# Two chunks of the output product in three rounded passes, with the parts of G made on the way

## The reference, cut to what matters

```python
queries = (query @ Wq + bq).reshape(B, L, H, E)        # H = 16 heads, E = 32
scores = jnp.einsum('blhe,bshe->bhls', queries, keys)  # 32 keys, the same for every b
A = sparsemax(scale * scores)
out = jnp.einsum('bhls,bshd->blhd', A, values)
out = jnp.transpose(out, (0, 2, 1, 3)).reshape(B, L, H * D)
x = layernorm(query + out @ Wo + bo)
# feed-forward: s = x @ Win + bin_; h = relu(s[..., None] * W1 + b1)
# g = einsum('btmh,mh->btm', h, W2) + b2
x = layernorm(x + g @ Wout + bout)
```

## Time and profile before

| What | Value |
|---|---|
| Median of 3 runs (lowest, highest) | 1313.4 us (1311.59, 1316.35) |
| Profiled execution: its own time | 1313.41 us |
| Its span, first to last instruction | 1311.6 us |
| Mean granted TensorE clock | 0.983 of full |
| Busy: TensorE, VectorE, ScalarE, GpSimd | 1248.0, 1133.2, 1068.2, 676.5 us |
| DMA: bytes moved, mean rate | 258 MB, 197 GB/s |

### The profile page before, as it was taken

How to read it: one execution, slowest core, us unless ns; L and a number is a source line. 1 busy time by engine, 2 the same in 40 slices (tenths; PEclk the granted TensorE clock), 3 DMA queues, 4 the chain that set the end, 5 groups by cost and what they waited for, 6 DMA issues and landing times. The chain is left out here.

```text
span 1311.6 us, 25223 instructions
## 1 busy us (share of the span) xinstructions
PE 1248.0 (95%) x5848; PEld 853.4 (65%) x5848; DVE 1133.2 (86%) x4538; ACT 1068.2 (81%) x2285; POOL 676.5 (52%) x1634
## 2 busy tenths in 40 slices
PE   8973899999999999999999999999999999989995
PEld 5642566676766767676776767677676767655552
DVE  3986899899999999999999999999999999966776
ACT  3661865779898888989898888989898888987776
POOL 1431333346555555655565555656555555665654
PEclk9995999999999999999999999999999999999998
DMA  6480785655656556565656656565655656468874
GB/s 203 131 215 17 199 246 192 191 185 171 218 184 216 198 197 206 190 217 182 220 188 208 203 191 214 185 220 183 213 196 199 211 186 216 162 227 281 280 233 104
DMA packets 92181, 258.35 MB, mean 197 GB/s; under 512 B 16067, under 2 KB 16067, under 8 KB 75622
## 3 DMA queue, kind: packets, MB, share of 16 engines
q1 hardware_dynamic: 91862, 256.26, 60.0%
q10 hardware_dynamic: 144, 0.26, 0.1%
HBM read 206.13 MB, written 50.33 MB: 196 GB/s over the span
## 5 line engine op out<-in xcount | busy, mean ns | idle before, releaser
L856 PE MATMUL bank<-G_sb,pT 128*128 128x512 f32 x1024 | 462.5, 594 | 2.8 <-DMA G_sb<-G_of_heads 2.1
L856 PEld LDWEIGHTS bank<-G_sb,pT 128*128 128x128 f32 x1024 | 185.2, 191 | 188.6 <-issue 184.3
L1426 DVE SCALAR_TENSOR_TENSOR acc<-hinge,w2c,acc 128x512 f32<-128x512 f32 x210 | 157.1, 748 | 81.7 <-ACT hinge L1019 80.2
L541 POOL TENSOR_TENSOR shift_sq<-sum,per_row_sq 128x1 f32<-128x1 f32 x244 | 95.2, 390 | 252.4 <-DVE y_sb L1269 250.5
L1376 DVE MAX8 top<-bank 128x8 f32<-128x32 f32 x2048 | 211.8, 178 | 0.0
L749 PE MATMUL bank<-A_hi,xT_hi 128*128 128x512 f32 x512 | 203.3, 397 | 0.0
L751 PE MATMUL bank<-A_hi,xT_lo 128*128 128x512 f32 x512 | 202.7, 396 | 0.0
L750 PE MATMUL bank<-A_lo,xT_hi 128*128 128x512 f32 x512 | 202.6, 396 | 0.0
L1019 ACT ACTIVATE hinge<-s_sb,b1c,w1c 128x512 f32<-128x512 f32 x240 | 192.8, 806 | 0.0
L1075 ACT CAST xT_hi<-bank 128x512 fp32r<-128x512 f32 x127 | 74.1, 584 | 134.8 <-PE bank L751 134.8
L989 ACT ACTIVATE unread<-y_sb,shift_sq 128x512 bf16<-128x512 f32 x244 | 174.5, 715 | 7.7 <-POOL minus_mean L543 7.5
(11 more groups left out here) (164 smaller groups left out, 2461.7 us busy)
## 6 DMA issues: line engine op xcount, KB each, us to landing
G_sb<-G_of_heads SPq DMA_DIRECT2D x128, 1024.0 KB, 5.5
x_sb<-in_L_attn_query_dram SPq DMA_DIRECT2D x128, 256.0 KB, 4.7
y_sb<-in_L_attn_query_dram SPq DMA_DIRECT2D x256, 128.0 KB, 5.4
out_dram<-o_sb SPq DMA_DIRECT2D x230, 128.0 KB, 4.7
G_of_heads<-y_sb SPq DMA_DIRECT2D x64, 256.0 KB, 4.0
out_dram<-y_sb SPq DMA_DIRECT2D x11, 256.0 KB, 3.3
y_sb<-in_L_attn_Wk_dram SPq DMA_DIRECT2D x1, 1024.0 KB, 5.9
y_sb<-in_L_attn_Wq_dram SPq DMA_DIRECT2D x1, 1024.0 KB, 8.1
```

The source lines that it names most:

```text
L541: nc.gpsimd.tensor_tensor(shift_sq[:, par:par + 1], total[:, par:par + 1], per_row_sq[:], ALU.mult).then_inc(s_mean, 1)
L856: mm = nc.tensor.matmul(o_ps[i % 2][:], pT[:, bass.ds(pair_place(turn, i) + (i % H * C + c) * P, P)], G_sb[:, i % GR, c, :], start=(c == 0 ...
L1426: nc.vector.scalar_tensor_tensor(acc[:], hinge[:, k % HR, :], w2c[:, k:k + 1], acc[:], ALU.mult, ALU.add).then_inc(s_acc, 1)
```

## The change

The output product treats some of its four chunks like the score: high and low parts of float32r, in three passes. In tiles 0 to 15 no chunk, in tiles 16 to 31 chunk 1, in tiles 32 to 105 chunks 1 and 3, in tiles 106 to 127 none. For this

- GpSimd makes the parts of the probabilities, `part_hi` and `part_lo`, one slot ahead of the product (`LAG_PART` 22): a copy that rounds and a subtraction, of 128 columns per converted chunk. They stand behind the split and ahead of the means.
- G's parts are made once. While tiles 0 to 15 pass, GpSimd makes the high and the low part of chunk 1 of each head's G (`made_hi` ahead of the means, `made_lo` behind the folds, 512 columns each); with tiles 16 to 31 those of chunk 3. SP stores them to `G_of_heads` (512 KB a tile) one slot later, ahead of its load of G.
- A buffer of the ring has six columns of 512 and the ring three buffers. A load brings 1.0 MB (tiles 0 to 15 and 106 to 127), 1.25 MB (16 to 31) or 1.5 MB (32 to 105). Loads from tile 35 on are issued one slot earlier (`LAG_G` 21); earlier ones keep slot i + 22.
- To have the room, `pT` becomes a ring of 20 blocks (it was 32 blocks' worth), reused block by block (`blocks`), and several small tensors go or move into others; four of the memsets at the start go.
- `shift_sq` goes from the means: ScalarE's square takes minus_mean as bias at scale 1, and ve is var / D + eps in one tensor_scalar.

The diff, cut to its core:

```diff
 LAG_PROB = 9
-LAG_G = 22
+LAG_G = 21
+LAG_PART = 22
 LAG_XB = 22
...
-        GR, STAGES = 2, 2
+        GR, STAGES, SETS = 3, 2, 5
         x_sb = sb("x_sb", [P, XR, D])
         xT_hi = sb("xT_hi", [P, C, P], F32R)
...
+        pT = sb("pT", [P, SETS * C * HPC * P])
+        part_hi = sb("part_hi", [P, 2, 2 * P], F32R)
+        part_lo = sb("part_lo", [P, 2, 2 * P], F32R)
         sum1 = sb("sum1", [P, 2])
...
-        G_sb = sb("G_sb", [P, GR, C, D])
-        V_rep, VT_rep = G_sb[:, 0].rearrange("p c n -> p (c n)"), G_sb[:, 1, 0, :]
-        G_dram = nc.dram_tensor("G_of_heads", [H, P, C * D], F32, kind="Internal").ap()
+        G_sb = sb("G_sb", [P, GR, 6, D], F32R)
+        G_hi = sb("G_hi", [P, 2, D], F32R)
+        V_rep, VT_rep = pT[:, 0:H * P], pT[:, C * C * HPC * P:C * C * HPC * P + D]
+        G_COLS = ((1, "raw"), (3, "raw"), (0, "raw"), (2, "raw"), (1, "hi"), (1, "lo"), (3, "hi"), (3, "lo"))
+        G_dram = nc.dram_tensor("G_of_heads", [H, P, len(G_COLS) * D], F32, kind="Internal").ap()
...
-        def pair_place(turn, i):
-            return (turn + i // UNROLL) % 2 * (H * C * P)
+        blocks, spare = [{(n, c): n * C + c for n in range(C) for c in range(C)}], list(range(C * C, C * C + C))
+        for _ in range(1, TILES // UNROLL):
+            old = blocks[-1]
+            blocks.append({(n, c): old[c - 1, n] if c else spare[n] for n in range(C) for c in range(C)})
+            spare = [old[C - 1, c] for c in range(C)]
+        p_blocks = pT[:].rearrange("p (b a n) -> p b a n", a=HPC, n=P)
+        def block_of(i, c):
+            return blocks[i // UNROLL][i % H // HPC, c]
+        PARTS_MADE = (1, 3)
+        PLAIN_FROM = TILES - 22
+        def parts_of(i):
+            chunks = PARTS_MADE[:i // UNROLL] if i < PLAIN_FROM else ()
+            return sorted(chunks, key=lambda c: block_of(i, c))
+        def plain_of(i):
+            return [c for c in range(C) if c not in parts_of(i)]
+        def parts_before(i):
+            return sum(bool(parts_of(n)) for n in range(i))
+        def made_of(i):
+            return PARTS_MADE[i // UNROLL] if i // UNROLL < len(PARTS_MADE) else None
+        MADE_HI, MADE_LO = 4, 5
+        def made_hi(i):
+            return G_sb[:, i % GR, MADE_HI, :] if i < H else G_hi[:, i % 2, :]
+        def made_lo(i):
+            return G_sb[:, i % GR, MADE_LO, :]
+        def made_stores(i):
+            return sum(16 if n < H else 32 for n in range(i % GR, i + 1, GR))
+        def G_cols(i):
+            wanted = [G_COLS.index((c, "raw")) for c in plain_of(i)]
+            wanted += [G_COLS.index((c, part)) for c in parts_of(i) for part in ("hi", "lo")]
+            assert max(wanted) - min(wanted) + 1 == len(wanted)
+            return min(wanted), max(wanted) + 1
+        def G_of(i, c, kind):
+            return G_sb[:, i % GR, G_COLS.index((c, kind)) - G_cols(i)[0], :]
+        def parts_rows(i):
+            places = [block_of(i, c) for c in parts_of(i)]
+            if len(places) == 1:
+                return slice(places[0], places[0] + 1)
+            return slice(places[0], places[1] + 1, places[1] - places[0])
...
             AHEAD = 2
+            LAG_MADE = LAG_WO + 1
+            def G_loads(n):
+                return [i for i, early in ((n - LAG_G - 1, False), (n - LAG_G, True))
+                        if 0 <= i < TILES and early == (i >= len(PARTS_MADE) * H + GR)]
+            def store_made(i):
+                col = G_COLS.index((made_of(i), "hi"))
+                if i < H:
+                    sp.dma_start(G_dram[i % H, :, col * D:(col + 2) * D],
+                                 G_sb[:, i % GR, MADE_HI:MADE_LO + 1].bitcast(F32).rearrange("p c n -> p (c n)")
+                                 ).then_inc(s_made_st[i % GR], 16)
+                else:
+                    for n, part in enumerate((made_hi(i), made_lo(i))):
+                        sp.dma_start(G_dram[i % H, :, (col + n) * D:(col + n + 1) * D],
+                                     part.bitcast(F32)).then_inc(s_made_st[i % GR], 16)
             def slot(turn, j):
...
+                    i = base + j - LAG_MADE
+                    sp.wait_ge(s_made, i + 1)
+                    store_made(i)
+                for i in G_loads(base + j):
                     h = i % H
-                    if isinstance(turn, int) and base + i < H:
-                        if h == 0:
-                            sp.wait_ge(s_Gmm, PIECES)
-                        if h % HPC == 0:
-                            for r in range(STAGES):
-                                sp.wait_ge(s_Gst[r], 16 * HPC * (h // HPC + 1) * (C // STAGES))
-                    if not isinstance(turn, int) or base + i >= GR:
-                        sp.wait_ge(s_o, base + i - GR + 1)
-                    sp.dma_start(G_sb[:, i % GR].rearrange("p c n -> p (c n)"), G_dram[h]).then_inc(
-                        s_G[i % GR], 16)
+                    if i < H and h % HPC == 0:
+                        for r in range(STAGES):
+                            sp.wait_ge(s_Gst[r], 16 * HPC * (h // HPC + 1) * (C // STAGES))
+                    if i >= GR:
+                        sp.wait_ge(s_o, i - GR + 1)
+                        if made_of(i - GR) is not None:
+                            sp.wait_ge(s_made_st[i % GR], made_stores(i - GR))
+                    first, last = G_cols(i)
+                    sp.dma_start(G_sb[:, i % GR, 0:last - first].bitcast(F32).rearrange("p c n -> p (c n)"),
+                                 G_dram[h, :, first * D:last * D]).then_inc(s_G[i % GR], 16)
                 if in_range(turn, j, LAG_XB):
                     i = j - LAG_XB
...
-            def mean(t0, par, s_rows, total, s_mean, minus_mean, shift_sq, s_shift):
+            def mean(t0, par, s_rows, total, s_mean, minus_mean, s_shift):
                 if not isinstance(t0, int) or t0 >= 3:
                     pool.wait_ge(s_shift, t0 - 2)
                 pool.wait_ge(s_rows, t0)
-                nc.gpsimd.tensor_tensor(shift_sq[:, par:par + 1], total[:, par:par + 1], per_row_sq[:],
-                                        ALU.mult).then_inc(s_mean, 1)
                 nc.gpsimd.tensor_tensor(minus_mean[:, par:par + 1], total[:, par:par + 1], per_row[:],
                                         ALU.mult).then_inc(s_mean, 1)
...
                 pool.wait_ge(s_ve, t0)
                 nc.gpsimd.tensor_tensor(rstd[:, par:par + 1], ve[:], minus_half[:], ALU.pow).then_inc(s_rstd, 1)
-                pool.wait_ge(s_mean, 2 * t0)
+                pool.wait_ge(s_mean, t0)
                 pool.wait_ge(s_rstd, t0)
...
                     pool.wait_ge(s_lo, lead // GROUP + 1)
+                if in_range(turn, j, LAG_PART) and parts_of(base + j - LAG_PART):
+                    i = base + j - LAG_PART
+                    rows = p_blocks[:, parts_rows(i), i % HPC, :]
+                    hi, lo = (part[:, i % 2, 0:len(parts_of(i)) * P].rearrange("p (c n) -> p c n", n=P)
+                              for part in (part_hi, part_lo))
+                    pool.wait_ge(s_p, i // UNROLL * UNROLL + 3 * GROUP + i % H // HPC + 1)
+                    pool.wait_ge(s_o, i - 1)
+                    nc.gpsimd.tensor_copy(hi, rows).then_inc(s_phi, 1)
+                    pool.wait_ge(s_phi, parts_before(i) + 1)
+                    nc.gpsimd.tensor_tensor(lo, rows, hi.bitcast(F32), ALU.subtract).then_inc(s_plo, 1)
+                if in_range(turn, j, LAG_WO) and made_of(base + j - LAG_WO) is not None:
+                    i = base + j - LAG_WO
+                    pool.wait_ge(s_G[i % GR], 16 * (i // GR + 1))
+                    if i >= 2:
+                        pool.wait_ge(s_made_st[(i - 2) % GR], made_stores(i - 2))
+                    nc.gpsimd.tensor_copy(made_hi(i), G_of(i, made_of(i), "raw").bitcast(F32)).then_inc(s_made_hi, 1)
                 if in_range(turn, j, LAG_NORM1):
                     i = j - LAG_NORM1
...
                     fold(s_above, base + i + 1, above, s_folds)
+                if in_range(turn, j, LAG_WO) and made_of(base + j - LAG_WO) is not None:
+                    i = base + j - LAG_WO
+                    pool.wait_ge(s_made_hi, i + 1)
+                    nc.gpsimd.tensor_tensor(made_lo(i), G_of(i, made_of(i), "raw").bitcast(F32),
+                                            made_hi(i).bitcast(F32), ALU.subtract).then_inc(s_made, 1)
...
+            def output_product(i):
+                o, plain, in_parts = o_ps[i % 2], plain_of(i), parts_of(i)
+                for c in plain:
+                    mm = nc.tensor.matmul(o[:], p_blocks[:, block_of(i, c), i % HPC, :], G_of(i, c, "raw").bitcast(F32),
+                                          start=(c == plain[0]), stop=(not in_parts and c == plain[-1]))
+                if in_parts:
+                    pe.wait_ge(s_plo, parts_before(i) + 1)
+                for n, c in enumerate(in_parts):
+                    hi, lo = (part[:, i % 2, n * P:(n + 1) * P] for part in (part_hi, part_lo))
```

(22 more changed lines are left out.)

71 lines of the change are left out of this document (31 added, 40 removed).

## The result

| | before | after |
|---|---|---|
| Median (lowest, highest) | 1313.2 us (1311.59, 1316.35), 4 runs | 1299.44 us (1298.62, 1300.57), 4 runs |
| Profiled execution, its span | 1313.41, 1311.6 us | 1299.52, 1297.5 us |
| Ratio to before, 95% interval | | 0.9893 (0.9873 to 0.9913) |
| DMA bytes, mean rate | 258 MB, 197 GB/s | 318 MB, 245 GB/s |

The change makes the kernel 13.8 us faster. The forecast was 6 us faster.

A forecast was written before the change was run, and what follows sets the result against it. TensorE's own order was taken as the bound, about 3 us in 36.8 over the next engine. Span 1311.6 - 26.3 + 11.0 + 10.5 - 2.1 = 1304.7; with 1.8 around it 1306.5, stated as 1307 us, range 1291 to 1325.

The forecast's parts named there:

- The passes: Output product on TensorE: each converted chunk saves 0.16 us, 164 chunks 26.3 us (0.15 to 0.17 per chunk).
- What the saving meets in slots 55 to 128: ScalarE nearly bounds two slot intervals of four; 0.61 us lost per group, 18 groups, 11.0 of the 23.7 us saved.
- the rejected step: TensorE's transpose of y in the split-carrying slot needs the y ScalarE makes in that same slot, 0.07 us to spare.
- The square's lateness: Split-carrying slot: GpSimd's new copy and subtraction delay the mean, so ScalarE's square starts 0.41 us late; 0.36 lost per group.
- The parts of G: Slots 23 to 54: GpSimd's made_hi and made_lo delay mean and norms, so o_sb and y; 10.5 us, bounds 5 and 25.
- five holds of 0.45: Five groups making G's parts: 0.45 us added to each for VectorE held beside GpSimd, summed as 2.1 us.
- The count that only B pays: From slot 35, made_lo's 1.15 us delay of o_sb hides in ordinary slots (1.29 spare), but not after the split-carrying slot.
- rival 2: First two sets cost more than the rest brings: made_lo holds o_sb in every slot, 24 us not 10.5; 1320 us, chance 0.22.
- Rival 1: Saving arrives nearly whole, square not late; 4.5 us lost into split-carrying slots, first sets 5: 1294 us, chance 0.14.
- Rival 3: VectorE, held by GpSimd's new copy and subtraction, becomes the bound; the 23.7 us are gone: 1324 us, chance 0.10.
- The ring, the loads: Tail: three buffers remove TensorE's waits for G, -2.1 us; main part's DMA 0.76 to 0.8 busy, its loads hidden.
- own signs of being wrong: Chunk saving not 0.16; groups after slot 55 at 35.6 or above 36.7; slots 35 to 54 over 8 us more, no relief.

The follow-up runs named there:

- Experiment 7: Kernel before with one spare ScalarE pass ahead of o_sb in each split-carrying slot (one of four), slots 58 to 126: 1312.03 us, ratio 0.9985.
- experiment 6: Changed kernel with one, two or three spare ScalarE passes ahead of o_sb in each split-carrying slot, slots 58 to 126: 1304.88, 1318.52, 1332.4 us.
- experiment 9: Changed kernel with shift_sq back in both means, one more one-column GpSimd instruction in each: 1305.72 us, ratio 0.9944.
- experiment 1: Changed kernel with no chunk in parts; ring of three, earlier loads, shorter mean and block ring stay: 1308.67 us, ratio 0.9972.

## Why the prediction was right or wrong

- **The passes**: right. 0.16 per chunk was expected, and a group gives 1.33 for eight chunks, 0.166 each.
- **"What the saving meets in slots 55 to 128"**: this step failed. It took 11.0 us off the saving of 23.7; in slots 58 to 126 the full 22.1 arrived, to within 1 us. It said of the transpose of y "it needs the normalised y that ScalarE ends at 644.18 in slot A", and found 0.07 us to spare. The first norm has lags 24 and 25 and the transposes have lag 26, as the kernel's description itself says, so the y of slot A is transposed in B, a whole slot later. Two near times (644.18 and 644.25) had been taken for a wait that no view lists. Experiment 7 shows that on the kernel before (no loss at 0.66 us late), experiment 6 on the changed one. By the rejected step, one, two and three passes would have cost 11.7, 23.4 and some 35 us. They cost 5.4, 19 and 33 (of it 5.5, 17.8 and 31.3 in slots 58 to 126), by other waits: one and two mostly in slot C, and in A only where yT came later than its reader wanted it.
- **The square's lateness**: right as a time (0.37, forecast 0.41), though by other pieces. The copy took 0.74 in A beside u_sb (forecast 0.45), whose 1.72 us had begun before it. It is harmless because yT in the next slot, B, has 2.0 us to spare. More lateness from GpSimd is not: one more small instruction per mean cost 3.5 us in slots C (experiment 9), so little more lateness would have had a price.
- **"The parts of G"**: the mechanism was right up to o_sb, but its last link, to the transposes of y, was the rejected step again (yT and `differs` are what TensorE waited for). The size was too small: 15.7 us against 10.5, inside the bounds of 5 and 25. The copy was cheaper than taken (0.61 to 0.66, forecast 0.80) and the subtraction dearer (1.33 to 1.38, forecast 1.26). (The forecast's five holds of 0.45 make 2.25 and not 2.1, which changes nothing.) The count that only B pays was wrong, and that was rival 2's claim: o_sb waited for the shift 13 times in some 16 slots, slots A, B and C all grew, and four groups took 39.5 to 39.9 where 38.5 was forecast. Rival 2 priced its case at 24 and decided from a subtraction of 1.4. The truth lies between it and the forecast. It could not decide the sign, since the 22.1 us of the later slots arrived.
- **Rival 1**, the saving arriving nearly whole, had 1294, and 0.14 as its chance. In slots 58 to 126 it is what happened, though even its own loss of 4.5 from D to A didn't come. It was held to be unlikely for the square's lateness in slot A, whose price experiments 6 and 7 refute. Its 5 us for the first sets were as far off as the forecast's, so its 1294 is below the measured time.
- **Rival 3**, VectorE as the bound: did not happen, but the rest fell from 2.9 to 1.3 us, and experiment 6 shows it in slot C. The next saving on TensorE would meet VectorE first.
- **The ring, the loads**: -3.5 with the shorter mean and the rest of the change (experiment 1) against -2.1. The part from slot 127 on gave 4.1, with parts or without; DMA was 0.93 busy at 304 GB/s between 1200 and 1250. The main part's DMA share is 0.78 to 0.88 (forecast 0.76 to 0.80), and costs nothing.

Together: 4.5 us worse in the first sets, 10.5 better in slots 58 to 126, 1.4 better at the end, make 7.4, which is within rounding the 7.2 us between the forecast span of 1304.7 and 1297.5. That the time fell inside the stated 1291 to 1325 is in part luck: two errors of opposite sign, 4.5 and 10.5, partly cancelled. The prediction's own signs of being wrong both showed: groups after slot 55 at 35.6 or less (35.47 measured), and more than 8 us lost in the first sets (12.1 in slots 39 to 57).

## What to carry to other kernels

Two times that nearly meet in a trace are no wait: before a margin goes into a sum, follow the data by its lag to the slot in which it is read, look whether the list of waits has that pair at all, and test a doubtful margin with one spare instruction in the kernel before. What counts is the distance from the end of an output to its first true reader (here 1.85 us for yT), for every chain that the late engine feeds. Work given to a slack engine belongs in one of its recorded waits: the same subtraction cost about 10 us more ahead of the norms than in a gap of the split, and 13 us more where it was so late that a store waited for it with the next load behind.

## What the runs showed of the hardware

In the kernel after, GpSimd's rounding copy to fp32r took 0.61 us for 512 columns (0.66 on average in the first set) and 0.50 on average for 256. The subtraction of the low part took 1.33 to 1.38 and 0.75. VectorE's tensor_scalar on a hinge took 1.50 beside such a subtraction, and 0.52 otherwise, here the first line against GpSimd's L720 at 438.53 above; its accumulation took 1.39 against 0.74:

```profile
438.61 1.50 DVE L1534 TENSOR_SCALAR acc<-hinge,w2c,b2c 128x512 f32<-128x512 f32 x1 [0.57 <-ACT hinge L1131]
...
448.14 1.39 DVE L1538 SCALAR_TENSOR_TENSOR acc<-hinge,w2c,acc 128x512 f32<-128x512 f32 x1 [0.25 <-ACT hinge L1131]
449.65 0.74 DVE L1538 SCALAR_TENSOR_TENSOR acc<-hinge,w2c,acc 128x512 f32<-128x512 f32 x1
```

The tensor_scalar has one tensor as its input, and the hold lasts about until GpSimd's instruction ends (439.83), which I had not reckoned with for such an instruction. The Trainium skill (SBUF — State Buffer, Who interferes with whom) names tensor_scalar among the operations that can enter a two-port mode and then exclude GpSimd for the whole instruction. By that rule, the trace agrees. Small GpSimd instructions are longer beside VectorE, too: rstd, on one column, took 1.05 us at 440.33, while VectorE's accumulation ran from 440.23 to 440.97, and 0.55 at 442.16.
